# Layer 0 attention: VectorE's reciprocal after the second pair of reductions, a step's first projection after its first scores

## The chip, the cores and the metric

The kernel runs as one program on one core of a Trainium2 chip. The metric is device time in microseconds of one execution, the median of several. The core has five engines that run their own instruction streams: TensorE (PE in the profile, with its weight loads listed apart as PEld), VectorE (DVE), ScalarE (ACT), GpSimd (POOL) and SyncE (SP), which issues most of the DMAs. They meet only at semaphores.

## The reference, cut to what matters

The program is two transformer layers. The change touches only the attention of layer 0, on x of shape (32, 256, 128), with 16 heads and a latent width L of 36:

```
xn   = layernorm(x)
kv   = xn @ latent_w + latent_b                       # (b, 256, 36), keys and values
q    = einsum('btc,hcl->bhtl', xn, Wd_w) + Wd_b       # 16 heads
s    = einsum('bhtl,bsl->bhts', q, kv) / sqrt(8)
attn = softmax(where(causal, s, -inf))
y    = einsum('bhts,bsl->bhtl', attn, kv)
x   += y.transpose.reshape(b, t, 16 * 36) @ out_w + out_b   (+ a routed FFN on the same xn)
```

Then follow the FFN of layer 0 and all of layer 1, which the change does not touch.

## The kernel before

**A step.** One batch element b is one step of the attention, 32 in all (0 to 31). The 16 heads are 8 pairs j (two heads lie in partitions 0 to 35 and 64 to 99), and two pairs form a group g (4 groups). A step works on three batch elements at once: it finishes the softmax of b, prepares the next one n = b + 1, and projects the output of q = b - 2. Steps 2 to 29 are the loop at L1964, two steps in a turn; the others are written out before and behind it.

**What PE does in a step** (`step`, L1888), in this order:

- `outp(q)` L1869: the output projection of b - 2 in bankB, 10 matmuls of 128 x 128 (L1874, L1876). It uses all the columns and more than 64 rows of the array.
- `qproj(n, 1)` L1814: the queries of pairs 2 and 3 of n in bankA, two matmuls over 128 rows (L1818). ACT copies them out with `qevac` (L1498, into `qT`), and POOL rounds them to bf16 with `round_queries` (L646, into `qb`).
- `smax(n, j)` L1822: scores of pair j from the bf16 copies, used only for the row maxima: four short matmuls (L1829, L1831) into bankS, on rows 0 to 35 and rows 64 to 99. It waits until `qb` of its pair is there, and, from the second pair on, until DVE has reduced the pair before it (`red_done`), since all pairs use the same bank.
- `st_first(b, g)` and `st_second(b, g)` L1834, L1844: the true scores of b in f32, transposed, into the four banks of bankT (L1841, L1847), on rows 0 to 36 and 64 to 100. From the second group on, `st_first` waits until ACT has taken the group before out of bankT (`exp_done`).
- `av(b, g)` L1851: attention times values, on two halves of the columns (L1861, L1865).

The step goes outp(q), qproj 1, smax 0, st_first 0, st_second 0, smax 1, qproj 2, st_first 1, smax 2, st_second 1, av 0, smax 3, qproj 3, and so on. It ends with smax 7, av 3, the keys and values of n + 1 (`kv`, L1809, L1811) and `qproj` of its first two pairs.

**The others.** ACT: `qevac(n, 1)`, then `probs(b, 0)` (two exponentials, L1503 and L1505), `qevac(n, 2)`, `probs(b, 1)`, and so on. POOL: `round_keys`, `round_queries(n, 0)`, two indirect DMAs (L629), then `clip(b, 0)` (the causal mask on the exponentials, L653 twice) and only behind it `round_queries(n, 1)`, which gives `qb` of pairs 2 and 3. DVE: `resid(q)` (L977), then `red(n, j)` for the eight pairs (L947 twice, L950 twice, each with a short read of the accumulator, `mneg`), with `invert(p)` and the three `normalise(p, i)` of p = b - 1 between them. `invert` (L963) waits for a DMA that brings the denominators (`dq`). SP then writes the reciprocals out (L381), reads them back broadcast (L387, L389), and `normalise` (L970) waits for these.

The order is written out by hand; there is no scheduler.

Of the kernel before, what the change touches and what calls it, by code (L numbers as in the profile page):

```python
# [36 lines left out]
def program(nc, a, out):  # L37
# [27 lines left out]
    with ctx:  # L65
# [248 lines left out]
        def passed(eng):  # L314

            eng.sem_inc(S["passed"], 1)
# [603 lines left out]
        def _(dve):  # L920
# [22 lines left out]
            def red(n, j):  # L943
                dve.wait_ge(S["s_ps"], n.b * PAIRS + (j + 1))
                passed(dve)
                for e in range(2):
                    dve.tensor_tensor_reduce(masked[:, e, 0:P], bankS[:, e, 0:P], causal[:, P:2 * P], -1.0, -NEG, ALU.add, ALU.min,  # L947
                                             mneg[:, n.half, e, j, 0:1])
                for e in range(2):
                    ins = dve.tensor_tensor_reduce(masked[:, e, P:3 * P], bankS[:, e, P:3 * P], causal[:, :], -1.0, -NEG, ALU.add, ALU.min,  # L950
                                                   mneg[:, n.half, e, j, 1:2])
                ins.then_inc(S["red_done"], 1)

            def turn_maxima(n, prior):
                dve.wait_ge(S["red_done"], n.b * PAIRS + PAIRS)
                if prior:
                    dve.wait_ge(S[f"m_in{n.half}"], n.pair * 64)
                passed(dve)
                dve.transpose(mT[:, n.half, :], mneg[:, n.half].rearrange("p e j t -> p (e j t)")).then_inc(S["mT_sb"], 1)

            def invert(p):
                dve.wait_ge(S["den_in"], p.b * 16 + 16)
                dve.reciprocal(rq[:, :], dq[:, :]).then_inc(S["rec_done"], 1)  # L963

            def normalise(p, i):
                if i == 0:
                    dve.wait_ge(S["zrows_in"], p.b * NZ + NZ)
                if i < QUADS // 2:
                    rows = yT[:, p.half, 2 * i:2 * i + 2, :]
                    dve.tensor_tensor(rows, rows, rzb[:, 2 * i:2 * i + 2, :], ALU.mult)  # L970
                else:
                    dve.tensor_tensor(yR[:, p.half, :], yR[:, p.half, :], rzr[:, :], ALU.mult).then_inc(S["z_done"], 1)

            def resid(p):
                dve.wait_ge(S["out_ps"], p.b + 1)
                rows = xa_all[:, bass.ds(p.b * 2, 2), :]
                dve.tensor_tensor(rows, bankB[:, 0:2 * C].rearrange("p (t c) -> p t c", t=2), rows, ALU.add).then_inc(S["xa_done"], 1)  # L977

            def stage(b, prior):
                u = b.half  # L980
                if prior:
                    dve.wait_ge(S[f"scat{u}"], (b.pair - FIRST // 2) * 32)
                rows = bass.ds(b.b * 2 - FIRST, 2)
                dve.tensor_copy(stage_x[:, u], xn_all[:, rows, :])
                dve.tensor_copy(stage_p[:, u, :], pos_all[:, rows]).then_inc(S["staged"], 1)
# [87 lines left out]
            def step(n, p, q, staged, prior=True):  # L1073
                if staged:
                    stage(staged, prior)
                if q:
                    resid(q)
                if n:
                    red(n, 0)
                if p:  # L1080
                    invert(p)
                if n:
                    red(n, 1)
                    red(n, 2)
                    red(n, 3)
                    red(n, 4)
                if p:
                    normalise(p, 0)
                if n:
                    red(n, 5)  # L1090
                    red(n, 6)
                if p:
                    normalise(p, 1)
                if n:
                    red(n, 7)
                    turn_maxima(n, True)
                if p:
                    normalise(p, 2)
# [59 lines left out]
            places(3)  # L1158
            places(4)
            step(Batch(1, 1), second, first, None)  # L1160
            kv(Batch(2, 0))
            gates0()
# [613 lines left out]
        def _(pe):  # L1776
# [37 lines left out]
            def qproj(n, r):  # L1814
                if r:
                    pe.wait_ge(S["q_sb"], n.b * PAIRS + 2 * r)
                for k in range(2):
                    ins = pe.matmul(bankA[:, k * T:(k + 1) * T], wd[:, 2 * r + k, :, :].rearrange("p e l -> p (e l)"),  # L1818
                                    xnT[:, n.half, :], start=True, stop=True)
                ins.then_inc(S["q_ps"], 1)  # L1820

            def smax(n, j):  # L1822
                pe.wait_ge(S["qb_sb"], n.b * PAIRS + (j + 1))
                if j == 0:
                    pe.wait_ge(S["kb_sb"], n.b + 1)
                else:
                    pe.wait_ge(S["red_done"], n.b * PAIRS + j)
                for e in range(2):
                    pe.matmul(bankS[:, e, 0:P], qb[ROWS[e], j, 0:P], kb[ROWS[e], 0:P], start=True, stop=True, skip_group_check=True)  # L1829
                for e in range(2):  # L1830
                    ins = pe.matmul(bankS[:, e, P:3 * P], qb[ROWS[e], j, P:T], kb[ROWS[e], :], start=True, stop=True, skip_group_check=True)  # L1831
                ins.then_inc(S["s_ps"], 1)

            def st_first(b, g, prior):  # L1834
                u = b.half
                if g == 0:
                    pe.wait_ge(S[f"m_in{u}"], b.pair * 64 + 64)
                if prior:
                    pe.wait_ge(S["exp_done"], b.b * (2 * GROUPS) + 2 * g)
                for e in range(2):  # L1840
                    pe.matmul(bankT[:, e, :], kT[KEYS[e], u, 0:P], qT[KEYS[e], u, 2 * g:2 * g + 2, :].rearrange("p j t -> p (j t)"),  # L1841
                              start=True, stop=True, skip_group_check=True)
# [26 lines left out]
            def outp(p, t, free):  # L1869
                if t == 0:  # L1870
                    pe.wait_ge(S["z_done"], p.b + 1)
                    pe.wait_ge(S["y_sb"], free)
                for j in range(QUADS):
                    pe.matmul(bankB[:, t * C:(t + 1) * C], yT[:, p.half, j, t * P:(t + 1) * P], ow[:, j, :],  # L1874
                              start=(j == 0), stop=False)
                ins = pe.matmul(bankB[:, t * C:(t + 1) * C], yR[:, p.half, t * P:(t + 1) * P], owr[:, :], start=False, stop=True)  # L1876
                if t:
                    ins.then_inc(S["out_ps"], 1)

            def rank(k, weights):  # L1880
                pe.wait_ge(S["te_go"], 1)
                if k == 0:
                    pe.wait_ge(S["y_sb"], GROUPS)
                else:
                    pe.wait_ge(S["rk_sb"], 2)
                pe.matmul(bankB[:, :], weights[:, :], oh0[:, :, :].rearrange("p n e -> p (n e)"), start=True, stop=True).then_inc(S["rk_ps"], 1)

            def step(b, n, q, m, prior, ranks=False):  # L1888
                if q:
                    outp(q, 0, b.b * GROUPS)  # L1890
                    outp(q, 1, None)
                if ranks:
                    rank(0, onesb)
                if n:
                    qproj(n, 1)
                    smax(n, 0)
                if ranks:
                    rank(1, strict)
                st_first(b, 0, prior)
                st_second(b, 0)  # L1900
                for g in range(1, GROUPS):
                    if n:
                        smax(n, 2 * g - 1)
                        if g < GROUPS - 1:
                            qproj(n, g + 1)
                    st_first(b, g, True)
                    if n and g < GROUPS - 1:
                        smax(n, 2 * g)
                    st_second(b, g)
                    if n and g == GROUPS - 1:  # L1910
                        smax(n, 2 * g)
                    av(b, g - 1, "ranks" if ranks else q is not None)
                if m:
                    xnt(m, None, True)
                if n:
                    smax(n, PAIRS - 1)
                av(b, GROUPS - 1, True)
                if m:
                    pe.wait_ge(S["red_done"], n.b * PAIRS + PAIRS)
                    kv(m)  # L1920
                    qproj(m, 0)
# [391 lines left out]
```

## Time and profile before

| | |
|---|---|
| median of 3 runs | 1747.52 us (1747.44 to 1747.92) |
| the profiled execution's own time | 1746.09 us |
| its span, first to last instruction | 1744.6 us |
| PE / PEld / DVE / ACT / POOL busy, share of the span | 86 / 62 / 66 / 57 / 53% |
| PE busy in 200 to 700 us, the attention's steps | 97.5% |
| DVE / ACT / POOL busy there | 59 / 54 / 50% |
| granted TensorE clock in 200 to 700 us | 1.00 |
| granted clock in 60 to 100 us, before and in step 0 | 0.50 |
| rzb<-reciprocals (L387), issue to landing, median | 2.6 us |

The steps of the attention fill the time from about 95 to 807 us. Busy time of PE is counted from the start of a matmul to its modelled end, and matmuls overlap, so a share of 97% does not say that nothing is lost: the distance between the starts of two matmuls tells more than their durations. A matmul of f32 operands stands in the trace as two records, so two of them read "x4". A time in square brackets behind a row is idle time of the engine before it, and what ended it.

### The profile page before, as it was taken

What the parts mean: (1) busy time and instruction counts of PE and PEld (TensorE: products, weight loads), DVE (VectorE), ACT (ScalarE), POOL (GpSimd) and SP (SyncE); (2) the same over time, 40 slices, a digit from 0 to 9 for tenths busy, and PEclk for the clock granted to TensorE, in tenths of its full rate; (3) what the DMA queues carried; (4) which work ended last, traced back from release to release, by engine and by line L of the source; (5) the groups of instructions that cost most, each with busy time, mean ns of one, the idle gap of its engine ahead of it and who ended that gap; (6) DMA issues with size and microseconds to landing.
All of it is one profiled execution on the core that took longest, in us unless ns stands there. A gap on an engine that the chain in (4) does not pass through costs nothing.

```text
span 1744.6 us, 44545 instructions
## 1 busy us (share of the span) xinstructions
PE 1504.7 (86%) x13025; PEld 1078.0 (62%) x13027; DVE 1146.8 (66%) x4175; ACT 997.4 (57%) x2526; POOL 920.7 (53%) x1625
## 2 busy tenths in 40 slices
PE   4798999999999999998997588888888888885883
PEld 4644555555555555546997477777777777764772
DVE  3356655555555555553654498998989989976561
ACT  3344555555555555553332688888888888852341
POOL 5234555554544554553444566666666666632663
PEclk8579999999999999999999699999999999996666
DMA  7402222222222222223332111211112121116444
GB/s 196 134 19 69 56 55 56 56 55 54 55 55 55 55 55 56 56 61 85 69 69 55 23 44 44 45 42 41 44 44 45 42 41 44 44 29 128 84 91 113
DMA packets 240882, 107.55 MB, mean 62 GB/s; under 512 B 145465, under 2 KB 229242, under 8 KB 240762
## 3 DMA queue, kind: packets, MB, share of 16 engines
q1 hardware_dynamic: 230586, 93.23, 22.3%
q0 software_dynamic: 10240, 13.64, 3.7%
q8 instruction: 26, 0.43, 0.1%
q14 instruction: 30, 0.25, 0.0%
HBM read 61.92 MB, written 40.16 MB: 59 GB/s over the span
## 4 chain that ended last, share of the span: by engine, by line
PE 59%; ACT 18%; issue 7%; POOL 6%; DVE 5%; DMA 3%; SPq 1%; POOLq 1%; DVEq 0%; ACTq 0%
PE bankB L1861 7%; PE bankA L1818 6%; PE bankT L1841 5%; PE bankT L1993 4%; PE bankT L1847 3%; PE bankB L1874 3%; PE bankB L1865 3%; ACT qx L1602 3%; ACT km L1611 2%; ACT gqx L1602 2%; PE bankT L2112 2%; PE bankS L1829 2%; ACT probs L1503 2%; PE bankA L2094 2%; ACT rows L1675 2%
## 5 line engine op out<-in xcount | busy, mean ns | idle before, releaser
L653 POOL TENSOR_SCALAR_AFFINE_SELECT probs<-probs 128x512 f32<-128x512 f32 x256 | 176.6, 713 | 225.6 <-ACT probs L1503 225.6
L947 DVE CUSTOM_DVE_ANT_0 masked<-bankS,causal 128x128 bf16<-128x128 f32 x512 | 127.9, 287 | 178.7 <-PE bankS L1831 177.7
L1503 ACT ACTIVATE probs<-bankT 128x1024 f32<-128x1024 f32 x128 | 131.1, 1024 | 134.5 <-PE bankT L1847 134.5
L1498 ACT ACTIVATE qT<-bankA,bd 128x256 f32<-128x256 f32 x256 | 107.5, 471 | 159.3 <-PE bankA L1818 155.6
L950 DVE CUSTOM_DVE_ANT_0 masked<-bankS,causal 128x256 bf16<-128x256 f32 x512 | 195.6, 420 | 0.1
L1818 PE MATMUL bankA<-xnT,wd 128*128 128x256 f32 x512 | 147.2, 411 | 1.9 <-ACT qT L1498 1.9
L1841 PE MATMUL bankT<-qT,kT 37*128 37x512 f32 x512 | 143.4, 637 | 2.4 <-ACT probs L1505 2.2
L1861 PE MATMUL bankB<-probs,vaug 128*64 128x512 f32 x512 | 140.8, 628 | 3.3 <-ACT yT L1510 0.9
L1307 DVE STREAM_TRANSPOSE pt<-pe 128x768 f32<-128x768 f32 x128 | 124.4, 972 | 26.4 <-ACT pe L1588 26.2
L2112 PE MATMUL bankT<-vx,pt 128*64 128x68 f32 x1024 | 72.6, 228 | 55.9 <-ACT gkm L1631 55.9
L1588 ACT ACTIVATE pe<-pr 128x768 f32<-128x768 f32 x128 | 108.0, 844 | 7.2 <-DVE pr L1301 4.8
L646 POOL CAST qb<-qT 128x256 bf16<-128x256 f32 x256 | 96.0, 400 | 28.9 <-ACT qT L1498 28.7
L1510 ACT COPY yT<-bankB 128x512 f32<-128x512 f32 x128 | 75.0, 586 | 61.4 <-PE bankB L1865 61.4
L1818 PEld LDWEIGHTS bankA<-xnT,wd 128*128 128x128 f32 x512 | 90.3, 197 | 21.4 <-issue 12.7
L1829 PEld LDWEIGHTS bankS<-kb,qb 36*128 36x128 bf16 x512 | 27.2, 93 | 115.8 <-issue 65.0
L2112 PEld LDWEIGHTS bankT<-vx,pt 128*64 128x64 f32 x1024 | 55.7, 137 | 68.6 <-ACT gkm L1631 36.3
L716 POOL COPY probs<-wall 128x516 f32 x72 | 45.0, 625 | 78.0 <-DVE qT L1193 75.4
L753 POOL DMA_INDIRECT yg<-ys_sorted,idx_g x64 | 65.7, 1027 | 37.0 <-POOL gate_g L749 25.7
L1865 PEld LDWEIGHTS bankB<-probs,vaug 128*64 128x64 f32 x512 | 37.5, 139 | 75.0 <-issue 66.5
L1993 PE MATMUL bankT<-wall,qT 128*128 x576 | 78.9, 280 | 0.1
L1865 PE MATMUL bankB<-probs,vaug 128*64 128x256 f32 x512 | 78.5, 385 | 0.0
L1847 PE MATMUL bankT<-qT,kT 37*128 37x256 f32 x512 | 77.7, 380 | 0.0
(307 smaller groups left out, 4257.1 us busy)
## 6 DMA issues: line engine op xcount, KB each, us to landing
rzb<-reciprocals SPq DMA_DIRECT2D x128, 128.0 KB, 2.6
yT<-yT SPq DMA_DIRECT2D x64, 128.0 KB, 2.3
xtab<-tab SPq DMA_DIRECT2D x32, 192.0 KB, 2.0
xs_sorted<-zeros SPq DMA_DIRECT2D x1, 4608.0 KB, 18.5
qT<-xs_sorted SPq DMA_DIRECT2D x144, 32.0 KB, 1.8
ys_sorted<-qT SPq DMA_DIRECT2D x36, 128.0 KB, 1.9
value_rows<-vrow SPq DMA_DIRECT2D x32, 128.0 KB, 1.8
vx<-value_rows SPq DMA_DIRECT2D x256, 16.0 KB, 1.8
```

The lines of the kernel that those rows point to most:

```text
L653: pool.affine_select(out=blocks, in_=blocks, compare_op=ALU.is_ge, fill=0.0, base=0, pattern=[[0, 4], [1, P]], channel_multiplier=-1).then ...
L947: dve.tensor_tensor_reduce(masked[:, e, 0:P], bankS[:, e, 0:P], causal[:, P:2 * P], -1.0, -NEG, ALU.add, ALU.min, mneg[:, n.half, e, j, 0:1])
L950: ins = dve.tensor_tensor_reduce(masked[:, e, P:3 * P], bankS[:, e, P:3 * P], causal[:, :], -1.0, -NEG, ALU.add, ALU.min, mneg[:, n.half, ...
L1307: dve.transpose(pt[:, g].rearrange("p k b g q -> p (k b g q)"), pe1[:, g % 2].rearrange("p k s q -> p (k s q)")).then_inc(S["tr_done"], 1)
L1503: act.activation(pT[:, g % 2].rearrange("p e j t -> p e (j t)"), bankT[:, 0:2, :], ACT.Exp, scale=SCALE0).then_inc(S["exp_done"], 1)
L1818: ins = pe.matmul(bankA[:, k * T:(k + 1) * T], wd[:, 2 * r + k, :, :].rearrange("p e l -> p (e l)"), xnT[:, n.half, :], start=True, stop=True)
L1841: pe.matmul(bankT[:, e, :], kT[KEYS[e], u, 0:P], qT[KEYS[e], u, 2 * g:2 * g + 2, :].rearrange("p j t -> p (j t)"), start=True, stop=True, ...
L1847: ins = pe.matmul(bankT[:, 2 + e, 0:T], kT[KEYS[e], u, P:T], qT[KEYS[e], u, 2 * g:2 * g + 2, P:T], start=True, stop=True, skip_group_check ...
L1861: pe.matmul(bankB[HALVES[e], :], vaug[:, u, 0, :], pT[:, g % 2, e].rearrange("p j t -> p (j t)"), start=True, stop=False, skip_group_check ...
L1865: ins = pe.matmul(bankB[HALVES[e], :].rearrange("p (j t) -> p j t", t=T)[:, :, P:T], vaug[:, u, 1, :], pT1[:, g % 2, e], start=False, stop ...
L1993: ins = pe.matmul(bankY[u][:, 0:C], hT[:, u, k, :], wall[:, bass.ds(e, 1), F0 + KF + k * C:F0 + KF + (k + 1) * C].rearrange("p a c -> p (a ...
L2112: pe.matmul(slots_ps[DL * k:DL * (k + 1), n, 0:PW], pt[:, g, 1, k, 2 * (n % 2):2 * (n % 2) + 2, :].rearrange("p g q -> p (g q)"), vx[:, u, ...
```

## The change

Two lines move in PE's step and one in DVE's. On PE, `qproj(n, 1)` goes from ahead of `smax(n, 0)` to behind it (in step 1 also behind the `rank(1, ...)` matmul of the router). On DVE, `invert(p)` goes from behind `red(n, 0)` to behind `red(n, 1)`. Nothing is added or taken away, and no wait changes.

```diff
@@ DVE, step(n, p, q, staged, prior) @@
                 if n:
                     red(n, 0)
+                    red(n, 1)
                 if p:
                     invert(p)
                 if n:
-                    red(n, 1)
                     red(n, 2)
@@ PE, step(b, n, q, m, prior, ranks) @@
                 if n:
-                    qproj(n, 1)
                     smax(n, 0)
                 if ranks:
                     rank(1, strict)
+                if n:
+                    qproj(n, 1)
                 st_first(b, 0, prior)
                 st_second(b, 0)
```

On PE, at the head of the second step in the loop's body, the rows that differ (L1874 and L1876 are outp, L1829 and L1831 smax 0, L1818 qproj 1, L1841 and L1847 the f32 scores):

```order
 L1874 MATMUL bankB<-ow,yT 128x128 x4
 L1876 MATMUL bankB<-owr,yR 128x128
+L1823 REGISTER_ALU
+L1829 MATMUL bankS<-kb,qb 128x128 x2
+L1831 MATMUL bankS<-kb,qb 128x256 x2
 L1816 REGISTER_ALU
 L1818 MATMUL bankA<-xnT,wd 128x256 x2
-L1823 REGISTER_ALU
-L1829 MATMUL bankS<-kb,qb 128x128 x2
-L1831 MATMUL bankS<-kb,qb 128x256 x2
 L1841 MATMUL bankT<-qT,kT 128x512 x2
```

The two short matmul groups of smax 0 stood between the projection and the f32 scores, and stand now between the output projection and the projection.

On DVE, in the same step, before (L950 ends red 0, L963 is invert, L947 opens red 1):

```order
L950 ISA masked,mneg<-bankS,causal 128x256
L950 ISA mneg 128x1
L962 ISA
L963 RECIPROCAL rq<-dq 128x32
L944 REGISTER_ALU
L947 ISA masked,mneg<-bankS,causal 128x128
```

and of the change, the same stretch:

```order
L944 REGISTER_ALU
L947 ISA masked,mneg<-bankS,causal 128x128
L947 ISA mneg 128x1
L947 ISA masked,mneg<-bankS,causal 128x128
L947 ISA mneg 128x1
L950 ISA masked,mneg<-bankS,causal 128x256
L950 ISA mneg 128x1
L950 ISA masked,mneg<-bankS,causal 128x256
L950 ISA mneg 128x1
L962 ISA
L963 RECIPROCAL rq<-dq 128x32
```

The whole of red 1 now stands ahead of the reciprocal and of its wait for the denominators.

## Rows read from the trace of the kernel before

**Rows 1.** Timeline of PE, head of step 14 (start, us, engine, line, operands, count, idle before):

```profile
412.74 0.39 PE L1876 MATMUL bankB<-owr,yR 80*128 80x128 f32 x2
412.96 1.03 PE L1818 MATMUL bankA<-xnT,wd 128*128 128x256 f32 x4
413.92 0.23 PE L1829 MATMUL bankS<-kb,qb 36*128 36x128 bf16 x2
413.99 0.27 PE L1831 MATMUL bankS<-kb,qb 36*128 36x256 bf16 x2
414.10 1.02 PE L1841 MATMUL bankT<-qT,kT 37*128 37x512 f32 x4
414.96 0.59 PE L1847 MATMUL bankT<-qT,kT 37*128 37x256 f32 x4
415.81 0.23 PE L1829 MATMUL bankS<-kb,qb 36*128 36x128 bf16 x2 [0.26 <-DVE mneg L950]
416.08 1.13 PE L1818 MATMUL bankA<-xnT,wd 128*128 128x256 f32 x4
417.17 1.13 PE L1841 MATMUL bankT<-qT,kT 37*128 37x512 f32 x4
418.51 0.23 PE L1829 MATMUL bankS<-kb,qb 36*128 36x128 bf16 x2 [0.21 <-POOL qb L646]
```

**Rows 2.** Timeline of ACT and POOL, the same stretch:

```profile
415.60 1.02 ACT L1503 ACTIVATE probs<-bankT 128x1024 f32<-128x1024 f32 x1 [0.74 <-PE bankT L1847]
416.52 0.59 ACT L1505 ACTIVATE probs<-bankT 128x512 f32<-128x512 f32 x1
...
416.80 1.22 POOL L653 TENSOR_SCALAR_AFFINE_SELECT probs<-probs 128x512 f32<-128x512 f32 x2 [1.74 <-ACT probs L1503]
417.97 0.74 POOL L646 CAST qb<-qT 128x256 bf16<-128x256 f32 x2
```

**Rows 3.** Timeline of PE, later in step 14: smax 3, qproj 3, st_first 2, smax 4:

```profile
420.72 0.27 PE L1831 MATMUL bankS<-kb,qb 36*128 36x256 bf16 x2
420.92 1.13 PE L1818 MATMUL bankA<-xnT,wd 128*128 128x256 f32 x4
421.98 1.13 PE L1841 MATMUL bankT<-qT,kT 37*128 37x512 f32 x4
422.95 0.22 PE L1829 MATMUL bankS<-kb,qb 36*128 36x128 bf16 x2
```

**Rows 4.** Timeline of PE's weight loads: those of st_first 0 and st_first 2:

```profile
413.99 0.30 PEld L1841 LDWEIGHTS bankT<-qT,kT 37*128 37x128 f32 x4
...
421.98 0.30 PEld L1841 LDWEIGHTS bankT<-qT,kT 37*128 37x128 f32 x4 [0.33 <-issue]
```

**Rows 5.** Timeline of DVE, head of step 14: resid, end of red 0, invert, end of red 1:

```profile
413.29 0.42 DVE L977 TENSOR_TENSOR xa_all<-bankB,xa_all 128x256 f32 x1 [2.04 <-PE bankB L1876]
...
415.58 0.08 DVE L950 DVE_READ_ACCUMULATOR2_ANT mneg<- 128x1 f32 x1
416.90 0.35 DVE L963 RECIPROCAL rq<-dq 128x32 f32<-128x32 f32 x1 [1.24 <-DMA dq<-remainders]
...
418.27 0.08 DVE L950 DVE_READ_ACCUMULATOR2_ANT mneg<- 128x1 f32 x1
```

**Rows 6.** Waits in 170 to 760 us, 27 steps (total us, times, longest):

```profile
PEld bankT L1841 <- ACT probs L1505: 9.8, 27, 0.4
...
PE bankS L1829 <- DVE mneg L950: 7.0, 28, 0.3
```

**Rows 7.** Timeline of POOL and PE, head of step 2:

```profile
149.26 0.75 POOL L646 CAST qb<-qT 128x256 bf16<-128x256 f32 x2
...
151.15 0.59 PE L1847 MATMUL bankT<-qT,kT 37*128 37x256 f32 x4
```

**Rows 8.** Timeline of SP's queue and DVE, step 14: last read of the reciprocals, normalise 0:

```profile
420.88 0.59 SPq L389 DMA_DIRECT2D rzr<-reciprocals  x1
...
424.59 0.69 DVE L970 TENSOR_TENSOR yT<-yT,rzb 128x512 f32<-128x512 f32 x1
```

## The prediction

> **What bounds the kernel now.** I read the page's table of slices and busy times first: in the attention PE is busy 97.5% of the time at full granted clock, and every other engine is under 60%. The reader is to see there only that PE is near its limit, not what a step loses. Then the timeline of PE over two steps, comparing starts. In a steady step PE really waits at two places near its head: smax 1 starts at 415.81, 0.26 us after the f32 scores ended, on DVE's first reduction, and smax 2 at 418.51, after 0.21 us, put down to POOL's `qb` [rows 1]. The table of waits says that the pattern is the rule: 27 steps, 27 waits of st_first 1's weight load on ACT, and 28 of smax on DVE [rows 6]. These are the waits that the two edits seem aimed at.
>
> Then the chain of waits, which ties them together. The second half of the f32 scores ends at 414.96 + 0.59 = 415.55; ACT starts the exponential at 415.60 and ends its second one at 416.52 + 0.59 = 417.11; POOL's mask starts at 416.80, and `qb` of pair 2 is the first of two casts from 417.97 on, so it ends at about 417.97 + 0.37 = 418.34 [rows 2]; smax 2 follows at 418.51 [rows 1]. So from the end of st_second 0 to smax 2 the head of the step is not set by PE, but by PE to ACT to POOL to PE. Meanwhile PE has only smax 1, qproj 2 and st_first 1 to do, and st_first 1 itself starts at 417.17, right behind the exponential's end at 417.11. What sets the length of a step is therefore (a) when st_second 0 ends, (b) that fixed chain, (c) PE's work behind smax 2.
>
> **The change part by part.**
>
> *red 1 ahead of the reciprocal (DVE).* Before, red 0 ends at 415.66, DVE waits for the denominators until 416.90, and red 1 begins behind the reciprocal and ends at 418.35 [rows 5]. That is as late as `qb` (418.34). After, red 1 starts when its scores are there and ends about 1.2 us later, near 417.4, and the reciprocal after it, at 417.4 instead of 416.90. What this gives is the time by which red 1 alone held smax 2. The profile puts 28 waits of smax on DVE in 27 steps [rows 6]: 27 are smax 1, so hardly more than one is smax 2, and red 1 is level with `qb` rather than behind it. Bounds: nothing, and 0.1 us a step, which is 2.7 us in all. I take 0.5 us in all, the low side, since POOL ends 27 other waits. Behind it the reciprocals are later by 0.5 us, of which 0.39 is the shift of the whole step (below). Their last DMA is issued at 420.88, lands some 2.6 us later at 423.5, and normalise 0 starts at 424.59 [rows 8] without waiting: 1.1 us of cover for 0.1 us. Cost zero.
>
> *smax 0 ahead of qproj 1 (PE).* Smax 0 ends 0.9 us earlier. Red 0 may then start when resid ends, 413.29 + 0.42 = 413.71 [rows 5], takes 1.2 us as now and ends at 414.9, before PE can reach smax 1. So smax 1's wait goes. But PE has in its place only the wait of st_first 1 for the exponential, which ends at 417.11 whatever smax 1 does. The 0.26 us are not gained, they move by two instructions.
>
> *What the swap costs.* The order of the same matmuls is not free, by the distances between their starts. Before, from the last of outp: L1876 to L1818 0.22, L1818 to L1829 0.96, L1829 to L1831 0.07, L1831 to L1841 0.11, L1841 to L1847 0.86, together 2.22 us [rows 1]. After, the sequence is outp, smax, qproj, st_first, and each pair of neighbours stands elsewhere in the trace. L1831 to L1818 takes 0.20 and L1818 to L1841 1.06, both at a place where nothing is waited for, and L1841 to its follower 0.97 [rows 3]. For outp to smax I have no row; leaving a matmul on all rows for one on a row half costs about 0.10 (L1818 to L1829 is 0.96 [rows 1], where three distances of 0.215 and a stream of 0.215 would make 0.86), so 0.22 + 0.10 = 0.32. Sum 0.32 + 0.07 + 0.20 + 1.06 + 0.97 = 2.62. The difference is 0.40; with the third decimal of the single records 0.39. The weight loads say why. That of st_first 0 starts at 413.99, together with L1831, under smax's matmuls; that of st_first 2, behind qproj, starts only at 421.98, together with its own matmul, after 0.33 us without a load [rows 3, 4]. A load is pulled ahead when the neighbours cut the array alike, and not when the cut changes. Before there is one change of cut between outp and st_first (projection to smax), after there are three.
>
> The Trainium skill, page "TensorEngine Tiling (Array Packing)", section Key Properties, says that changing the tiling mode, unlike changing the tile, drains TensorE. The late weight loads agree. By the drain of about 175 ns that the page "TensorE: Matmul & The Clock Gate" gives (Single matmul latency), two more drains would be an estimated 0.35 us a step; the sum above does not use it. The latter page also says, in its Part 2, that the next tile's weights load while the running matmul streams; taken without the first rule it makes the swap free, and that is the second rival.
>
> *Is the 0.39 on the path?* Yes: it is all ahead of st_second 0's end, item (a). ACT has cover (its copy of qproj 1 would end near 415.4, before the exponential at 415.6 + 0.39). POOL waited 1.74 us for the exponential [rows 2], so it has no other brake. The whole chain, smax 2 and everything behind it move by 0.39.
>
> *Bounds of the 0.39.* The part with rows (0.20 for 0.11, 1.06 for 0.96, 0.97 for 0.86, less what outp to qproj already was) is 0.29 when the step from outp to smax costs nothing more; it is 0.49 when that costs twice what I took.
>
> *The steps at the edges.* In step 2 POOL gives `qb` of pair 0 only at 149.26 + 0.38 = 149.64 [rows 7]; smax 0 would start 0.14 later, as smax 2 does behind `qb`, at 149.78, and L1847 at 149.78 + 0.07 + 0.20 + 1.06 + 0.97 = 152.08, against 151.15: 0.93 us. In step 0 the clock is 0.50, so its 0.39 may be 0.4 to 0.8; I take 0.5. Step 1 has the router's matmul between them and as many changes of cut before as after: 0. In step 30 POOL has four indirect DMAs ahead of the mask and sets the pace: 0 (0.39 if not). Step 31 has no n.
>
> *Sum.* 27 x 0.39 = 10.5, plus 0.93, plus 0.5, less 0.5: 11.4 us. The profiled execution took 1746.09, so 1757.5; the median of the runs is 1.4 us above it, which gives 1758.9 us.
>
> **The rivals.**
>
> *Faster: the waits go and are not replaced.* If smax 2 depended on red 1 alone, the wait of 0.21 with the 0.16 that st_first 1 lost by being late, and the 0.26 of smax 1, would go: about 0.63 a step, against 0.39 for the swap, net 0.24 x 27 = 6.5 us faster, 1741.0. For it: the waits on DVE are real. Against it: `qb` ends at 418.34 and the exponential at 417.11, neither depends on DVE. It would be right from the point where `qb` is ready before about 418.0.
>
> *No change: the swap is free.* Weight loads are hidden at the new seams and only red 1's relief stays: 0.5 us faster, 1747.0. Against it stands every st_first that follows a projection in the steps from 200 to 700 us: its load starts with its matmul, as in [rows 4], and its first two records are 0.1 us longer than those of st_first 0.
>
> *Slower by more: the reciprocals come too late.* Red 1 pushes them past normalise 0, and then each further tenth costs a tenth a step. It decides from 1.1 us of delay on; I find 0.1. If a step lost another 0.3 us so, it would be 8 us more, 1767.
>
> *Part of it.* The seam costs are real but half hidden (0.2 a step): 1753.
>
> **How the numbers follow.** Forecast 0.80; half hidden 0.07; free swap 0.06; faster 0.05; slower by more 0.02. The forecast's own range is 27 x (0.29 to 0.49) with the edges and the relief of up to 2.7 us: 1754 to 1762. With half hidden it begins at 1752.5. A change under 0.2%, 3.5 us, can't be told from none; so slower 0.88, same 0.07, faster 0.05.
>
> **What would show it.** In a steady step of the changed kernel: L1829 right behind outp; L1818 0.20 behind L1831; weight loads of L1818 and of the first L1841 not ahead of their matmuls; L1847 about 2.3 us behind smax 0's start; no wait of smax 1 on DVE; a longer wait of st_first 1 on ACT (0.7 instead of 0.36 on the load's row); smax 2 still 2.8 to 2.9 us behind the start of ACT's L1503; a period 0.37 to 0.39 us longer; red 1 ending about 1 us before smax 2, and the reciprocal without a wait for `dq`. I am wrong if L1841 starts as early behind outp as before (seams), or if smax 2 comes closer than 2.8 us behind L1503 (chain).

## The result, and the profile after

The changed kernel takes 1758.0 us (median of 11 runs, 1751.6 to 1760.5) against 1745.7 us (11 runs, 1739.4 to 1749.5): a ratio of 1.0063, with a 95% interval of 1.0047 to 1.0078. It is slower, by about 11 us by the ratio; the two medians lie 12.3 us apart. The forecast was 1758.9 us with a range of 1752.5 to 1762.0.

One run of this program scatters by some 0.3%. The traces scatter far less in the attention, so from here on I read a step's length from it: the start of ACT's first exponential (L1503) in step 3 and in step 29, divided by 26 steps. That is (745.50 - 173.84) / 26 = 21.99 us before, and (758.47 - 177.32) / 26 = 22.35 us after.

Below, a seam is a place where one matmul uses all rows of the array and its neighbour only one part of the rows (the prediction's change of cut). The head of step 14 on PE, after the change (the rows that answer to [rows 1] and, from 426.05 on, to smax 2):

```profile
419.98 0.39 PE L1876 MATMUL bankB<-owr,yR 80*128 80x128 f32 x2
420.30 0.23 PE L1829 MATMUL bankS<-kb,qb 36*128 36x128 bf16 x2
420.37 0.27 PE L1831 MATMUL bankS<-kb,qb 36*128 36x256 bf16 x2
420.57 1.13 PE L1818 MATMUL bankA<-xnT,wd 128*128 128x256 f32 x4
421.63 1.13 PE L1841 MATMUL bankT<-qT,kT 37*128 37x512 f32 x4
422.59 0.60 PE L1847 MATMUL bankT<-qT,kT 37*128 37x256 f32 x4
423.02 0.22 PE L1829 MATMUL bankS<-kb,qb 36*128 36x128 bf16 x2
423.08 0.27 PE L1831 MATMUL bankS<-kb,qb 36*128 36x256 bf16 x2
423.29 1.13 PE L1818 MATMUL bankA<-xnT,wd 128*128 128x256 f32 x4
424.80 1.13 PE L1841 MATMUL bankT<-qT,kT 37*128 37x512 f32 x4 [0.38 <-ACT probs L1505]
426.05 0.23 PE L1829 MATMUL bankS<-kb,qb 36*128 36x128 bf16 x2
```

From the last of outp to L1847 it is 422.59 - 419.98 = 2.61 us, where it was 2.22 [rows 1]. Smax 1 now starts without a wait, 0.43 us behind L1847, and PE then waits in front of L1841 for the exponential, where it lost only 0.03 us before (1.09 us from L1818 to L1841 in [rows 1], against 1.06 where nothing is waited for). The wait moved; it did not go.

The weight loads of the same stretch, which answer to [rows 4]:

```profile
420.57 0.73 PEld L1818 LDWEIGHTS bankA<-xnT,wd 128*128 128x128 f32 x4 [0.16 <-issue]
421.63 0.30 PEld L1841 LDWEIGHTS bankT<-qT,kT 37*128 37x128 f32 x4 [0.33 <-issue]
```

Both start together with their own matmul. Before, the load of L1841 started at 413.99, under smax 0.

ACT, POOL and DVE there, answering to [rows 2] and [rows 5]:

```profile
423.24 1.02 ACT L1503 ACTIVATE probs<-bankT 128x1024 f32<-128x1024 f32 x1 [0.66 <-PE bankT L1847]
424.16 0.59 ACT L1505 ACTIVATE probs<-bankT 128x512 f32<-128x512 f32 x1
...
424.43 1.22 POOL L653 TENSOR_SCALAR_AFFINE_SELECT probs<-probs 128x512 f32<-128x512 f32 x2 [2.13 <-ACT probs L1503]
425.60 0.74 POOL L646 CAST qb<-qT 128x256 bf16<-128x256 f32 x2
...
420.53 0.42 DVE L977 TENSOR_TENSOR xa_all<-bankB,xa_all 128x256 f32 x1 [2.04 <-PE bankB L1876]
420.87 0.28 DVE L947 CUSTOM_DVE_ANT_0 masked<-bankS,causal 128x128 bf16<-128x128 f32 x1
...
424.66 0.08 DVE L950 DVE_READ_ACCUMULATOR2_ANT mneg<- 128x1 f32 x1
424.66 0.35 DVE L963 RECIPROCAL rq<-dq 128x32 f32<-128x32 f32 x1
```

From the exponential to POOL's cast the chain is the same to a hundredth: L1503 to POOL's mask 1.19 (1.20 before), to `qb` 2.36 (2.37). Smax 2 follows L1503 after 2.81 us (2.91 in that step before, where red 1 was the later one by 0.01 us). Only its start is later. Red 1 is done at 424.74, 1.3 us ahead of smax 2, and the reciprocal no longer waits for the denominators.

In the table of waits, 170 to 770 us (27 steps), answering to [rows 6]:

```profile
PEld bankT L1841 <- ACT probs L1505: 21.2, 27, 0.8
PEld bankT L1841 <- issue: 17.9, 54, 0.3
```

The wait of smax on DVE has left the table. That of L1841's load on ACT has grown from 9.8 to 21.2 us, and its loads that could not be pulled ahead are 54, two in a step, where it was one.

**Where the time went.** From the exponential of step 0 to that of step 31 it is 689.3 us before and 699.8 after: 10.5 us more. Of these, 9.9 lie between the exponentials of steps 2 and 29 (27 steps), 0.9 ahead of that of step 2, and the rest, -0.3 in all, in steps 1 and 30. The two spans differ by 12.0 us. The exponential of step 0 is 2.4 us later: 0.5 of that arises in step 0 itself, and 2.0 lie ahead of it and are the clock. From 30.1 us on the matmuls of L1791 start 0.21 us apart in the changed kernel and 0.11 in the kernel before, whose matmuls keep full speed for some 2 us longer; at the L1818 behind them the changed kernel is 2.1 us late. Dve_only (below), without the PE edit, shows the same and is 2.2 us behind. Behind the exponential of step 31 the changed kernel is 1.0 us shorter; that part is untouched by the change, and dve_only is 4.2 us shorter there and pe_only 1.8 us longer, so a difference of this size says nothing.

### The profile page after: what moved, and what is told of

Read it like the earlier page. It is cut to its first block, busy times and chain, and to the rows that moved or that the text cites. A ratio compares the mean times of both kernels' runs of the same rounds, so it can differ in the third digit from the quotient of the medians.

```text
span 1756.6 us, 44545 instructions
## 1 busy us (share of the span) xinstructions
PE 1515.4 (86%) x13026; PEld 1084.2 (62%) x13027; DVE 1145.2 (65%) x4175; ACT 994.1 (57%) x2526; POOL 920.6 (52%) x1625
## 4 chain that ended last, share of the span: by engine, by line
PE 59%; ACT 18%; issue 7%; POOL 6%; DVE 5%; DMA 2%; SPq 1%; POOLq 1%; DVEq 0%; ACTq 0%
PE bankB L1861 7%; PE bankA L1818 6%; PE bankT L1841 6%; PE bankT L1994 4%; PE bankT L1847 3%; PE bankB L1865 3%; PE bankB L1874 3%; ACT qx L1602 3%; ACT km L1611 2%; ACT gqx L1602 2%; PE bankS L1829 2%; PE bankB L2057 2%; ACT probs L1503 2%; PE bankS L1983 2%; PE bankT L1983 2%
## 5 line engine op out<-in xcount | busy, mean ns | idle before, releaser
L947 DVE CUSTOM_DVE_ANT_0 masked<-bankS,causal 128x128 bf16<-128x128 f32 x512 | 128.4, 288 | 224.7 <-PE bankS L1831 223.8
L1503 ACT ACTIVATE probs<-bankT 128x1024 f32<-128x1024 f32 x128 | 131.1, 1024 | 139.3 <-PE bankT L1847 139.3
L950 DVE CUSTOM_DVE_ANT_0 masked<-bankS,causal 128x256 bf16<-128x256 f32 x512 | 195.5, 419 | 0.2
L1841 PE MATMUL bankT<-qT,kT 37*128 37x512 f32 x512 | 147.8, 654 | 13.3 <-ACT probs L1505 13.1
L1818 PE MATMUL bankA<-xnT,wd 128*128 128x256 f32 x512 | 150.8, 419 | 0.0
L1818 PEld LDWEIGHTS bankA<-xnT,wd 128*128 128x128 f32 x512 | 90.8, 197 | 23.4 <-issue 15.8
L1829 PEld LDWEIGHTS bankS<-kb,qb 36*128 36x128 bf16 x512 | 26.2, 93 | 94.2 <-POOL qb L646 51.1
L1847 PE MATMUL bankT<-qT,kT 37*128 37x256 f32 x512 | 78.5, 384 | 0.0
```

Source lines behind the costliest of these rows:

```text
L1503: act.activation(pT[:, g % 2].rearrange("p e j t -> p e (j t)"), bankT[:, 0:2, :], ACT.Exp, scale=SCALE0).then_inc(S["exp_done"], 1)
L1847: ins = pe.matmul(bankT[:, 2 + e, 0:T], kT[KEYS[e], u, P:T], qT[KEYS[e], u, 2 * g:2 * g + 2, P:T], start=True, stop=True, skip_group_check ...
```

## The experiments

Each has one edit against one of the two kernels. "Period" is the length of a step as above.

| kernel | L1503 of step 3, step 29 | period | ratio to before, 95% |
|---|---|---|---|
| before | 173.84, 745.50 | 21.99 | |
| changed | 177.32, 758.47 | 22.35 | 1.0063 (1.0047 to 1.0078) |
| dve_only | 176.23, 747.27 | 21.96 | 1.0000 (0.9983 to 1.0016) |
| pe_only | 177.44, 758.68 | 22.36 | 1.0081 (1.0062 to 1.0100) |
| pool_only | 173.58, 745.04 | 21.98 | 0.9995 (0.9979 to 1.0012) |
| pool_dve | 175.48, 738.94 | 21.67 | 0.9938 (0.9917 to 0.9958) |
| all_three | 176.81, 750.80 | 22.08 | 1.0005 (0.9990 to 1.0020) |
| rows_late | 172.49, 746.34 | 22.07 | one run |
| full_early | 175.78, 749.79 | 22.08 | one run |
| full_late | 176.69, 755.59 | 22.26 | one run |
| rows_early | 177.35, 756.15 | 22.26 | one run |
| covered | 177.00, 758.13 | 22.35 | one run |

### The two edits apart: dve_only and pe_only

```diff
# dve_only, against the kernel before
                     red(n, 0)
+                    red(n, 1)
                 if p:
                     invert(p)
                 if n:
-                    red(n, 1)
# pe_only, against the kernel before
-                    qproj(n, 1)
                     smax(n, 0)
                 if ranks:
                     rank(1, strict)
+                if n:
+                    qproj(n, 1)
```

> The kernel before with the DVE edit alone (invert behind red 1). Theory (the cost is PE's order, the DVE edit is nearly free): period of steps 3 to 29 between 21.94 and 21.98 us against 21.987 before (only the few hundredths by which red 1 held smax 2 go), smax 2 at 2.81 us behind the start of ACT's first exponential in every step, red 1 ending about 1 us earlier; 0.3 to 0.8 us off the whole, not to be told from no change. Rival (late reciprocals or a new wait on DVE cost the 12 us): period about 22.35, 10 us slower. Rival (DVE held smax 2): period 21.6, 10 us faster.

> The kernel before with the PE edit alone (qproj 1 behind smax 0). Theory (seams): period of steps 3 to 29 at 22.35 to 22.38 us, as in the changed kernel (22.352), L1847 0.39 us later behind outp than before, smax 1 without a wait on DVE, 10 to 11 us slower than before. Since the denominators now arrive 0.39 us earlier in the step, red 1 should not hold smax 2 even without the DVE edit. Rival (both edits together make the cost): period near 21.99, no change.

Dve_only: period 21.96, smax 2 at 2.81 to 2.82 us behind L1503 in all 27 steps (2.81 to 2.93 before). Red 1 ends early and the step goes on as it was:

```profile
419.73 0.08 DVE L950 DVE_READ_ACCUMULATOR2_ANT mneg<- 128x1 f32 x1
419.73 0.35 DVE L963 RECIPROCAL rq<-dq 128x32 f32<-128x32 f32 x1
...
417.87 1.02 ACT L1503 ACTIVATE probs<-bankT 128x1024 f32<-128x1024 f32 x1 [0.74 <-PE bankT L1847]
...
420.69 0.23 PE L1829 MATMUL bankS<-kb,qb 36*128 36x128 bf16 x2
```

Red 1 is done at 419.81 and smax 2 starts at 420.69: 0.9 us of lead, worth 0.02 us a step. Pe_only: period 22.36, the whole loss. So PE's edit alone makes the loss, and DVE's edit neither costs nor gives more than 0.03 us a step. Smax 2 stands at 2.81 to 2.82 us in pe_only too, as expected: with the swap the denominators are early enough, and in a steady step DVE's edit adds nothing to it. It matters in step 30, where in pe_only DVE waits 3.25 us for the denominators and red 1 then holds smax 2 for 1.07 us. Late reciprocals as the cause are out. Against dve_only, which has the same small relief, the swap costs 22.352 - 21.963 = 0.389 us a step.

### What holds smax 2: pool_only, pool_dve, all_three

```diff
# pool_only against before; pool_dve adds dve_only's edit, all_three adds both edits
-                clip(b, 0)
                 if n:
                     round_queries(n, 1)
+                clip(b, 0)
                 if m:
                     fetch_rows(m)
```

> The kernel before with POOL's round_queries(n, 1) ahead of clip(b, 0) instead of behind it, so that qb of pair 2 no longer hangs on ACT's exponential; DVE and PE as before. Theory (two things hold smax 2 at the same time, qb at 418.34 and red 1 at 418.35 in step 14): smax 2 stays where it is, now put down to DVE; period 21.9 to 22.0, no change. Rival (qb alone is the wait): period 21.6, 10 us faster.

> Both releasers of smax 2 moved: POOL's round_queries(n, 1) ahead of clip(b, 0), and DVE's invert behind red 1; PE as before. Theory: smax 2 follows st_first 1 without a wait, 0.37 us earlier (2.45 us behind the start of ACT's first exponential instead of 2.81 to 2.9); period 21.6, and 10 us (0.6%) faster than before. Rival (the exponential and PE's own work already set the step, the wait of smax 2 was harmless): period 21.95, no change.

> The changed kernel (both edits) with POOL's round_queries(n, 1) ahead of clip(b, 0) as well. Theory: the gain at smax 2 and the seams' cost add up, since the seams lie ahead of the exponential and the wait of smax 2 behind it: period 21.67 + 0.38 = 22.04 to 22.07 us, 1 to 2 us slower than before in all, not to be told from no change. Rival (with qb early, smax 1 being early too lets PE work the seams off): period 21.7, 8 to 10 us faster than before.

Pool_only: `qb` of pair 2 is now there 2.9 us earlier, and the period does not move (21.98 for 21.99), because red 1 stands right behind it: smax 2 is on average 2.83 us behind L1503 (2.84 before). With DVE's edit as well, both releasers are out of the way:

```profile
413.93 1.02 ACT L1503 ACTIVATE probs<-bankT 128x1024 f32<-128x1024 f32 x1 [0.74 <-PE bankT L1847]
...
413.39 0.74 POOL L646 CAST qb<-qT 128x256 bf16<-128x256 f32 x2
415.12 1.22 POOL L653 TENSOR_SCALAR_AFFINE_SELECT probs<-probs 128x512 f32<-128x512 f32 x2 [0.99 <-ACT probs L1503]
...
415.49 1.13 PE L1841 MATMUL bankT<-qT,kT 37*128 37x512 f32 x4
416.45 0.23 PE L1829 MATMUL bankS<-kb,qb 36*128 36x128 bf16 x2
```

POOL casts in the gap in which it used to wait for ACT, and smax 2 follows L1841 after 0.96 us, PE's own pace. The period falls to 21.67, and this kernel beats both: 0.6% faster than before. The two waits were in parallel; either edit alone gives 0.01 to 0.02 us a step, both together 0.32. My expectation had 21.6 and 2.45 us; I had taken the 0.37 us of step 14, where smax 2 was at 2.91, from the 2.81 of the typical step. It is 2.53.

All_three: 22.08, which is 21.67 + 0.41. The seams' cost comes back in full on top of the gain, a little more than the 0.37 to 0.40 expected. PE being early at smax 1 does not work it off, since L1841 of st_first 1 still waits for the exponential.

### The seam by itself: four kernels with a probe

One matmul of a single column is added in each step that has an output projection, in four combinations: cutting the array like smax (rows 0 to 35) or using all rows, and standing among row-cut neighbours (late) or among neighbours on all rows (early). Its result is not used.

```diff
# late: behind smax 0, ahead of st_first 0; early: ahead of qproj 1
+    probe_rows()  # pe.matmul(bankT[:, 0, 0:1], identb[0:L, :], identb[0:L, 0:1], ...)
+    probe_full()  # pe.matmul(bankT[:, 0, 0:1], identb[:, :], identb[:, 0:1], ...)
```

> The kernel before, plus one matmul of a single column (bf16, rows 0 to 35, 128 columns of weights, written to bankT and not used) between smax 0 and st_first 0 in each step with an outp: its neighbours cut the array as it does. Theory: no seam is added, period of steps 3 to 29 up by 0.02 to 0.08 us over 21.987. Rival (any matmul more, or any break in the order, costs the same wherever it stands): the four probe kernels show one and the same increase.

> The same probe on all 128 rows at the same place, between smax 0 and st_first 0 (two seams more). Theory: st_first 0's weight load is no longer pulled ahead; period up by 0.25 to 0.40 us. Rival: as in the kernel with the probe on rows 0 to 35.

> The probe on rows 0 to 35, between outp and qproj 1, whose neighbours use all rows (two seams more). Theory: qproj 1's first weight load is no longer pulled ahead; period up by 0.25 to 0.40 us. Rival: the same increase as at the other place.

> The probe on all 128 rows, between outp and qproj 1 (no seam more). Theory: period up by 0.02 to 0.08 us. Rival: as in the three other probe kernels.

| added to the period of 21.987 | among row-cut neighbours | among neighbours on all rows |
|---|---|---|
| probe on rows 0 to 35 | 0.084 (rows_late) | 0.275 (rows_early) |
| probe on all rows | 0.278 (full_late) | 0.090 (full_early) |

The same instruction costs 0.19 us more wherever it cuts the array unlike its neighbours, and it makes no difference which of the two forms it is. The rival, one price for any matmul more, is out. So is the number type: the probe is bf16 in all four, and at each place both forms have the same neighbours. The two prices without a seam are slightly above the 0.02 to 0.08 expected: the one weight load more stands in the way of the next f32 load. The loads around the probe, rows_late and then full_late (the columns are those of [rows 4]):

```profile
413.62 0.09 PEld L1892 LDWEIGHTS bankT<-identb 36*128 36x128 bf16 x1
413.63 0.40 PEld L1841 LDWEIGHTS bankT<-qT,kT 37*128 37x128 f32 x4
```

```profile
419.95 0.10 PEld L1889 LDWEIGHTS bankT<-identb 128*128 128x128 bf16 x1 [0.16 <-issue]
420.06 0.30 PEld L1841 LDWEIGHTS bankT<-qT,kT 37*128 37x128 f32 x4
```

In rows_late the probe's load starts with L1831 (413.62) and L1841's 0.01 us later. In full_late the probe's load starts 0.20 us behind L1831 (419.75), and L1841's 0.11 behind that.

### A seam where nothing waits for it: covered

```diff
# against the changed kernel, in smax(n, 1), behind its waits
+                if probe:
+                    pe.matmul(bankB[:, 0:1], identb[:, :], identb[:, 0:1], start=True, stop=True, ...)
```

> The changed kernel (both edits), plus the single-column probe on all 128 rows between st_second 0 and smax 1, its result in bankB unused: two seams more, but behind the start of ACT's exponential and ahead of st_first 1, which waits for that exponential. Theory (a seam costs only where it stands on the chain from outp to st_second 0): smax 1 starts about 0.3 us later, st_first 1 where it was, period of steps 3 to 29 within 0.02 us of the changed kernel's 22.352. Rival (seams cost PE their time wherever they stand, since PE is 97% busy): period 22.6 to 22.7.

```profile
422.27 0.60 PE L1849 MATMUL bankT<-qT,kT 37*128 37x256 f32 x4
422.80 0.18 PE L1829 MATMUL bankB<-identb 128*128 128x1 bf16 x1
422.91 0.23 PE L1831 MATMUL bankS<-kb,qb 36*128 36x128 bf16 x2
422.98 0.27 PE L1833 MATMUL bankS<-kb,qb 36*128 36x256 bf16 x2
423.18 1.13 PE L1818 MATMUL bankA<-xnT,wd 128*128 128x256 f32 x4
424.48 1.13 PE L1843 MATMUL bankT<-qT,kT 37*128 37x512 f32 x4 [0.17 <-ACT probs L1505]
```

(From the probe on, the program's lines are two further down: L1843 is the changed kernel's L1841.) Smax 1 starts 0.64 us behind st_second 0 instead of 0.43, so the two seams cost PE their 0.21. The wait for the exponential shrinks from 0.38 to 0.17 by the same 0.21, and the period is 22.351 against 22.352. Two seams cost the step nothing behind st_second 0, while ahead of st_first 0 the same probe made the step 0.28 us longer (full_late).

## Why the prediction was right

**The bound.** The step is set by the end of st_second 0, the chain ACT, POOL, PE, and PE's work behind smax 2. That held for the changed kernel: the chain kept its length, and covered shows the slack beside it. In the kernel before, the link over POOL to smax 2 was only one of two: pool_only took it away and the step kept its length, since red 1 ended as late. The prediction had read the two as level and still put smax 2 down to POOL; its sum does not depend on it. The part that held in every run is PE to ACT to st_first 1: L1841 starts 1.56 to 1.57 us behind L1503 in steps 3 to 29 of all twelve kernels here.

**The swap, 0.39 us a step.** Measured 0.39 from outp to L1847 (2.61 for 2.22), and 0.389 in the period against dve_only. The distances borrowed from other places in the step held one by one: outp to smax 0.32 (0.32, an estimate and the one distance without a row), L1831 to L1818 0.20, L1818 to L1841 1.06, L1841 to L1847 0.96 (0.97 taken). The probes show apart from this that the cause is the change of cut and not the order of these matmuls. What happens at a seam is less certain: the weight load is late and the first f32 matmul behind it longer, and no run tells whether the late load is the cause or follows from a wait at the seam. The Trainium skill's rule that a change of tiling mode drains TensorE (page "TensorEngine Tiling (Array Packing)", section Key Properties) agrees with all four probes. The prediction's estimate of 0.35 us, from the drain figure of the page "TensorE: Matmul & The Clock Gate" (Single matmul latency), was near the 0.39 measured. But one price for every seam does not fit the rows, as the last section shows.

**The edge steps.** Step 2: 0.88 measured (28.37 for 27.49 us between exponentials), 0.93 predicted, and smax 0 did wait for `qb`, 0.49 us. Step 0, against dve_only, where the clock was alike: from its qproj 0 to st_second 0 7.54 us for 7.06, so 0.48 for the 0.5 taken. That is in part luck: smax 0 waited 1.18 us for `qb` there, where qproj 1 had waited 1.02 for ACT, and the prediction had counted seams alone. Step 1: 0 taken, 0.2 us shorter in the trace (24.96 for 25.19); the kernels here take 21.8 to 25.6 us for it, and this is not explained. Step 30: its seams cost 0.38 up to its exponential and 0.46 were given back behind it, together about nothing. POOL takes 5.85 us from its cast of pairs 0 and 1 through its four DMAs to the mask in both kernels (763.40 to 769.25 before, 776.37 to 782.22 after), and smax 2 waits behind them for `qb`, so a later exponential costs nothing there.

**DVE's edit.** 0.5 us in all was predicted. Dve_only gives (21.987 - 21.963) x 27 = 0.6 us in the steady steps, and 0.4 from the exponential of step 0 to that of step 31 (689.0 for 689.3), invisible in the time. Its step 2 is 0.36 longer, by one late smax; rows_early, which does not have the DVE edit, shows the same jump of 0.35 at the same smax.

**The waits that went.** They were replaced as said: smax 1's by st_first 1's. The rival that they would be gained needed `qb` before 418.0. All_three supplies just that, with both edits in place, and is 0.09 us a step slower than before, not 0.24 faster. So the rival's price was wrong as well: of its 0.63 us only the part at smax 2 can be had, 0.32 in pool_dve, which pays no seams. The 0.26 of smax 1 can't, since st_first 1 waits for the exponential (0.38 us in all_three, as in the changed kernel).

**The total.** 11.4 us forecast over the profiled 1746.1; the trace shows 10.5 between the exponentials and 0.5 ahead of them, and the ratio says 11.0 us (8.2 to 13.6). That the time itself, 1758.0, came within 0.9 us of 1758.9 is in part luck: the kernel before had a median of 1747.5 us in the three runs that the forecast started from and 1745.7 in all eleven. The sum held by its terms, 27 x 0.39 above all.

## What to carry to other kernels

Read what an order costs from the distances between starts, each pair of neighbours at a place where it already stands; the same matmuls in another order were 0.39 us dearer, because it has two more changes between full and divided rows, at which no weight load is pulled ahead. Put such seams where the engine waits anyway. Where two releasers end within hundredths of each other, moving one gives next to nothing (0.01 and 0.02 us a step here, 0.32 for both): move both, and first look for one that stands behind a wait it does not need, as POOL's cast did behind the mask.

## What the hardware showed that I had not expected

- A seam's price depends on the weights behind it. By the distances, leaving rows in full for bf16 smax costs 0.10 us (0.31 from the last L1818 to L1829, for a stream of 0.215); going into f32 weights costs 0.19 to 0.20, half in the late load, half in the first f32 matmul, whose follower starts 0.32 instead of 0.22 us later. Three such seams less the one there was, 0.10 + 0.19 + 0.19 - 0.10, make 0.38 of the 0.39. Covered and rows_early bear it out: two seams that both lead into bf16 weights cost PE 0.21 us, and one into bf16 and one into f32 weights 0.30 (from L1876 to the second record of L1818, 0.63 for 0.33). In rows_early these 0.30, less the 0.02 that smax 2 gains as in dve_only, are all that the probe adds (0.275); without a seam the probe costs 0.09 by itself, and 0.19 is the difference.
- The granted clock of the profile can be wrong near the start. In dve_only it is given as 1.00 in 95 to 120 us, while four records of L1818 take 2.04 us there, at 96.10, and 1.03 in the steady steps: half speed. In the kernel before the same four records take 2.05 us at 94.02, and there the clock is given as 0.50. Durations decide.
